# An eight-batch attention and expert block on one core: another order of calls, value tiles filled on ScalarE, a cleared tile multiplied in early gaps

## The chip, the core and the metric

One core of a Trainium2 chip runs the whole block in one launch. The metric is the device time in microseconds (us) of an execution; a profile of one execution shows every instruction of the five engines: TensorE (PE, with its weight loads PEld), VectorE (DVE), ScalarE (ACT), GpSimd (POOL) and SyncE (SP). Each engine has its own queue and takes it in order; semaphores tie them together.

## The reference

The input is 8 batches of 256 tokens of 128 features, float32. Each batch is normalised (xn) and goes into two branches that are added to it:

```
xn  = layernorm(x)
A   = softmax(q k^T / sqrt(128)) ; y = A summed with v as written, fc, bias
out0 = layernorm(xn + y) * gamma + beta
h   = rms(xn) ; 16 heads of 8 ; q, k = rms per head
ao  = causal softmax(q k^T / sqrt(8)) v, projected by wo
x1  = xn + ao (features 32 to 127 only) ; xf = rms(x1)
w   = top-2 weights of softmax(xf gate^T) over 4 experts
out1 = x1 + w0 gelu(e0) + w1 silu*linear(e1) + w2 (three gelu layers) + w3 (two gelu layers)
x + out0 + out1
```

In the first branch the reference's einsum sums attention over its keys and values over their tokens apart, so that it is a row sum of the softmax times one projected vector (fc_row).

## The kernel before

All weights and all batches stay in SBUF. The work is cut into some 70 small steps of a batch n: Python functions, each of which emits the instructions of one engine with the waits that they need. For each engine one long list of calls, written out by hand, sets the order in which the steps of all 8 batches are mixed: `batches()` for TensorE and VectorE, plain lists for GpSimd and ScalarE. The lists keep two or three batches in flight.

The steps of a batch, in the order in which its data flows:

- VectorE `ln_statistics`, `ln_moments`; GpSimd `ln_variance`, `ln_pow` and, for the second scale, `h_square`, `h_mean`, `h_eps`, `h_pow`; VectorE `ln_normalise` makes xn. TensorE `x_turn` transposes it, ScalarE `x_copy` takes it out of PSUM.
- TensorE `qkv_project(n, j)` for the two halves of the tokens, ScalarE `qkv_copy`; GpSimd `v_copy` puts the values into a tile `v_aug`, 32 columns for a head: 8 values, then a column of ones. VectorE `qk_square`, `qk_mean`, `rsqrt_input`, `rsqrt_guess`, four `cubic_` and three `newton_` steps, `qk_norm`. TensorE `qk_turn`, ScalarE `q_copy` and four `k_copy`.
- For each of 4 groups g of 4 heads: TensorE `scores(n, g)`, ScalarE `exp_group(n, g)`, GpSimd `mask(n, g)` (128x1024 elements in place), TensorE `weigh_v(n, g)`. VectorE `pv_turn`, `heads_inverse`, `heads_divide`, `ao_turn`; TensorE `wo_project`; VectorE `residual`; ScalarE `x1_square`; GpSimd `x1_pow`; VectorE `residual_scale` makes xf.
- The first branch: TensorE `q0_project`, `a0_scores(n, j)`; VectorE `a0_max`; ScalarE `a0_softmax`; VectorE `a0_inverse`, `a0_weight`; TensorE `fc_row`; VectorE `h0_sum`, `h0_statistics`, `h0_moments`, `h0_norm`; GpSimd `biased` and `h0_variance` to `h0_add`, then `x1_add`, which completes acc.
- Experts: TensorE `xf_turn`, `gate`, `e1_first`, `e1_second`, `l1_layer`, `l2_layer`, `l3_layer`, `e0_up`, `e3_in`, `e3_up_layer`, with ScalarE's gelu or tanh behind each and VectorE's `e1_gate` and `e1_product`; the small gate steps on VectorE; TensorE `down(n, j)`, and VectorE's `down(n, j, e)`, which adds the four weighted experts into acc. SyncE stores acc.

Results of TensorE go to four PSUM banks that many steps share in turn, beside the four banks of the scores. A step claims its bank when the result before it in that bank has been read:

```
"QKV0": "a", "QKV1": "a", "QKT": "a", "PV0": "a", "PV1": "a",
"XT": "b", "Q0T": "b", "S00": "b", "S01": "b", "FC": "b", "XFT": "b", "GATE": "b", "WO": "b",
"E1A": "even", "L1": "even", "L2": "even", "L3": "even", "DN0": "even",
"E1B": "odd", "E0": "odd", "D3": "odd", "U3": "odd", "DN1": "odd",
```

(S00 and S01 are the results of `a0_scores`, PV0 and PV1 those of `weigh_v`, DN0 and DN1 those of `down`.) A second list of the same calls, for inputs whose scores could overflow, is skipped at run time by a flag that VectorE computes first (`bound_scores`).

Of the kernel before, what the change touches and what calls it, by code (L numbers as in the profile page):

```python
# [30 lines left out]
def fused_block(nc: bass.Bass, x, cols, rows, w_proj, w_first, w_up, w_mid, w_down, out):  # L31
# [15 lines left out]
    with ExitStack() as ctx:  # L47
# [122 lines left out]
        def _(pe):  # L170
# [260 lines left out]
            def batches():  # L431
                x_turn(0); qkv_project(0, 0); fold_weights(); q0_project(0); qkv_project(0, 1); a0_scores(0, 0)
                a0_scores(0, 1); x_turn(1); qk_turn(0); q0_project(1); find_maxima(0); scores(0, 0); x_turn(2)
                qkv_project(1, 0); scores(0, 1); qkv_project(1, 1); fc_row(0); scores(0, 2); a0_scores(1, 0)
# [2 lines left out]
                a0_scores(2, 0); scores(1, 1); qkv_project(2, 1); a0_scores(2, 1); scores(1, 2); weigh_v(1, 0)
                xf_turn(0); weigh_v(1, 1); scores(1, 3); gate(0); l1_layer(0); e3_in(0); weigh_v(1, 2); x_turn(4)
                weigh_v(1, 3); e1_first(0); e3_up_layer(0); qk_turn(2); wo_project(1); l2_layer(0); e0_up(0)
                fc_row(2); find_maxima(2); scores(2, 0); l3_layer(0); e1_second(0); xf_turn(1); qkv_project(3, 0)  # L440
                scores(2, 1); e3_in(1); gate(1); down(0, 0); down(0, 1); q0_project(3); scores(2, 2)
# [955 lines left out]
```

## Time and profile before

| | us |
|---|---|
| median of 3 runs | 233.01 (232.93 to 233.16) |
| the execution that was profiled | 233.21 |
| its span, first to last instruction | 231.5 |
| TensorE / ScalarE / VectorE / GpSimd busy in it | 199.3 / 170.2 / 153.4 / 107.7 |

The profile's rows give times in us from the start of the span. In the timeline, instructions of one line that follow each other are merged (x2), and the bracket tells how long the engine was idle before them and what ended it. A group's row gives the busy time, the mean duration in ns of one, and the idle time ahead of the group.

### The profile page before, as it was taken

To read this page: it belongs to the slowest core of one execution; us is meant where nothing else is said; L and a number is where in the kernel's file an instruction comes from. 1 tells how busy PE (TensorE), PEld (TensorE's weight loads), DVE (VectorE), ACT (ScalarE), POOL (GpSimd) and SP (SyncE) were. 2 spreads that over 40 slices of the span, in tenths; PEclk is the share of its full clock that TensorE was granted. 3 is DMA by queue.
4 is the path that set the end of the run, shared out by engine and by line. 5 is a ranking of instruction groups with operands and counts; after the bars stand their busy time and mean duration, and the time that the engine had idled before them with its cause. 6 is when DMAs were issued, how large, how long until landed. Compare 5 with 4: busy or idle time off the path is not lost. (4 is left out here: it accounts for less than half of the span.)

```text
span 231.5 us, 5985 instructions
## 1 busy us (share of the span) xinstructions
PE 199.3 (86%) x2132; PEld 145.4 (63%) x2132; DVE 153.4 (66%) x534; ACT 170.2 (74%) x288; POOL 107.7 (47%) x190
## 2 busy tenths in 40 slices
PE   0557765989999998898999899999999999969892
PEld 0325433656868765765777678667786786747682
DVE  6453489279837881597669486797479847843354
ACT  2225843778998989997989998899999677636610
POOL 6851587865381715251476266515622536720000
PEclk9985999599999999999999999999999999999999
DMA  5930000000000000000000000000000000000001
GB/s 130 385 97 1 4 0 0 3 1 3 0 1 3 25 0 0 3 25 1 1 3 27 0 0 3 27 0 4 0 25 0 4 0 25 3 0 0 1 3 52
DMA packets 5393, 5.00 MB, mean 22 GB/s; under 512 B 498, under 2 KB 4850, under 8 KB 5362
## 3 DMA queue, kind: packets, MB, share of 16 engines
q1 hardware_dynamic: 5072, 4.39, 5.8%
q8 instruction: 19, 0.31, 0.5%
q10 hardware_dynamic: 290, 0.20, 0.4%
q14 instruction: 12, 0.10, 0.1%
HBM read 3.54 MB, written 1.05 MB: 20 GB/s over the span
## 5 line engine op out<-in xcount | busy, mean ns | idle before, releaser
L563 POOL TENSOR_SCALAR_AFFINE_SELECT probs<-probs 128x1024 f32<-128x1024 f32 x32 | 35.3, 1102 | 49.2 <-ACT probs L724 48.9
L724 ACT ACTIVATE probs<-scores_ps 128x1536 f32<-128x1536 f32 x32 | 46.4, 1449 | 6.9 <-PE scores_ps L246 6.6
L246 PEld LDWEIGHTS scores_ps<-qT,kT 32*128 32x128 f32 x512 | 24.8, 195 | 15.4 <-issue 11.8
L246 PE MATMUL scores_ps<-qT,kT 32*128 32x128 f32 (+1 forms) x512 | 31.7, 363 | 3.1 <-ACT probs L724 3.0
L360 PE MATMUL even_ps<-l_h,mid 128*128 128x256 f32 x128 | 31.8, 391 | 1.1 <-DVE e_s L1029 1.1
L360 PEld LDWEIGHTS even_ps<-l_h,mid 128*128 128x128 f32 x128 | 23.0, 189 | 6.8 <-DVE e_s L1029 1.7
L778 ACT ACT_TABLE_LOAD x18 | 23.1, 1283 | 2.3 <-PE even_ps L360 1.8
L333 PE MATMUL odd_ps<-xfT,up 128*128 128x256 f32 x80 | 21.8, 387 | 0.2 <-DVE e_h L1040 0.2
L271 PE MATMUL a_ps<-probs,v_aug 128*32 128x256 f32 x256 | 20.3, 389 | 1.5 <-DVE pv_rows L1048 1.4
L778 ACT ACTIVATE l_h<-even_ps 128x512 f32<-128x512 f32 x24 | 14.4, 599 | 8.7 <-PE even_ps L360 6.8
L1235 DVE SCALAR_TENSOR_TENSOR acc<-even_ps,wts,acc 128x96 f32<-128x96 f32 x32 | 10.2, 318 | 14.2 <-PE even_ps L392 11.7
L333 PE MATMUL even_ps<-xfT,up 128*128 128x256 f32 x64 | 17.8, 400 | 0.4 <-DVE e_s L1029 0.2
L333 PEld LDWEIGHTS odd_ps<-xfT,up 128*128 128x128 f32 x80 | 14.5, 190 | 3.1 <-DVE e_h L1040 0.8
L216 PE MATMUL a_ps<-qkvT,xnT 128*128 128x384 f32 x32 | 15.2, 558 | 0.6 <-ACT xnT L742 0.6
L284 PE MATMUL b_ps<-xnT,q0T 128*128 128x256 f32 x32 | 11.2, 435 | 4.0 <-ACT a_exp L731 4.0
L731 ACT ACTIVATE a_exp<-b_ps,a_negmax 128x256 f32<-128x256 f32 x16 | 7.5, 472 | 9.1 <-DVE a_negmax L1122 9.1
L830 ACT ACTIVATE kT<-a_ps,k_rows 128x256 f32<-128x256 f32 x32 | 13.7, 493 | 0.0
L186 PE MATMUL b_ps<-ident,xn 128*128 128x128 f32 x16 | 4.0, 336 | 11.0 <-DVE xn L1222 8.1
L333 PEld LDWEIGHTS even_ps<-xfT,up 128*128 128x128 f32 x64 | 11.0, 189 | 3.4 <-ACT l_h L778 1.3
L724 ACT ACT_TABLE_LOAD x10 | 12.8, 1283 | 0.2
L275 PE MATMUL a_ps<-probs,v_aug 128*32 128x128 f32 x256 | 12.9, 273 | 0.0
L1048 DVE STREAM_TRANSPOSE pv_rows<-a_ps 128x512 f32<-128x512 f32 x16 | 11.3, 704 | 1.8 <-PE a_ps L275 1.8
(149 smaller groups left out, 433.3 us busy)
## 6 DMA issues: line engine op xcount, KB each, us to landing
x_sb<-in_x SPq DMA_DIRECT2D x8, 128.0 KB, 6.5
out<-acc SPq DMA_DIRECT2D x8, 128.0 KB, 1.8
mid<-in_mid SPq DMA_DIRECT2D x1, 640.0 KB, 7.4
up<-in_up SPq DMA_DIRECT2D x1, 578.0 KB, 6.3
downs<-in_down SPq DMA_DIRECT2D x1, 512.0 KB, 8.2
first<-in_first SPq DMA_DIRECT2D x1, 320.0 KB, 5.6
proj<-in_proj SPq DMA_DIRECT2D x1, 192.0 KB, 2.9
row<-in_rows ACTq DMA_DIRECT2D x1, 192.0 KB, 4.8
```

The source lines that it names most:

```text
L216: T.matmul(ps[:, 0:3 * D], xnT[n % X_COPIES][:, j * P:(j + 1) * P], qkvT[:], start=True, stop=True).then_inc(full_sem(fill), 1)
L246: ins = T.matmul(ps, kT[p][rows, g, kt * P:(kt + 1) * P], qT[p][rows, kt * P:SEQ], start=kt == 0, stop=kt == 1 and not searching, tile_pos ...
L271: T.matmul(rows, v_aug[p][:, 0, GROUPS * lane + g, :], probs[g][:, lane, 0:SEQ], start=True, stop=False, tile_position=(0, 32 * lane))
L275: ins = T.matmul(rows[:, P:SEQ], v_aug[p][:, 1, GROUPS * lane + g, :], probs[g][:, lane, SEQ:SEQ + P], start=False, stop=True, tile_positi ...
L284: T.matmul(ps, q0T[n % Q0_COPIES][:, j * P:(j + 1) * P], xnT[n % X_COPIES][:], start=True, stop=True).then_inc(full_sem(fill), 1)
L333: ins = T.matmul(ps[:, m * SEQ:(m + 1) * SEQ], wT[:, m * P:(m + 1) * P], xfT[n % XF_COPIES][:], start=True, stop=True)
L360: ins = T.matmul(ps[:, m * SEQ:(m + 1) * SEQ], wT[:, at_col:at_col + P], src[:, ci, :], start=(ci == 0), stop=(ci == HC - 1))
L563: nc.gpsimd.affine_select(out=own, in_=own, compare_op=ALU.is_ge, fill=0.0, base=0, pattern=[[0, LANES * TILES], [1, P]], channel_multipli ...
L724: nc.scalar.activation(probs[g][:, :, 0:SEQ + P], scores_ps[:, :, 0:SEQ + P], ACT.Exp).then_inc(s["exp_done"], 1)
L778: nc.scalar.activation(dst[n % 2][:].rearrange("p c q -> p (c q)"), ps_of(fill), ACT.Gelu).then_inc(read_sem(fill), 1)
L830: nc.scalar.activation(kT[n % HEAD_COPIES][:, g, :], ps_of("QKT")[:, SEQ:2 * SEQ], ACT.Copy, scale=k_rows[:, g:g + 1]).then_inc(s["k_copie ...
L1048: V.transpose(pv_rows[n % 2][:, 2 * pair:2 * pair + 2].rearrange("p g n e -> p (g n e)"), ps_of(fill)).then_inc(read_sem(fill), 1)
```

## The change

All four long lists are written anew. Beside that:

- The three value tiles were cleared and given their ones by VectorE (`clear_heads`); now ScalarE fills them whole with ones (`fill_heads`), and columns 9 to 31 of a head, which nobody uses, hold ones instead of zeros.
- VectorE clears a tile `spare` first of all, and TensorE multiplies it with itself into the odd bank (`keep_busy`): three times before the flag, and at four places early in its list, ten more. Nobody reads the result.
- The row constants (192 KB) are loaded by SyncE's queue behind x of batch 2 and no longer by ScalarE's queue; x of batch 4 is loaded ahead of mid and downs.

```
+            def keep_busy(count):
+                for _ in range(count):
+                    T.matmul(banks["odd"][:, 0:SEQ], spare[:, 0:P], spare[:], start=True, stop=True)
...
-                x_turn(0); qkv_project(0, 0); fold_weights(); q0_project(0); qkv_project(0, 1); a0_scores(0, 0)
-                a0_scores(0, 1); x_turn(1); qk_turn(0); q0_project(1); find_maxima(0); scores(0, 0); x_turn(2)
...
+                keep_busy(4); fold_weights(); x_turn(0); keep_busy(1); qkv_project(0, 0); x_turn(1); qkv_project(0, 1)
+                q0_project(0); qkv_project(1, 0); a0_scores(0, 0); qkv_project(1, 1); keep_busy(3); x_turn(2)
+                keep_busy(1); q0_project(1); qkv_project(2, 0); a0_scores(0, 1); qk_turn(0); fc_row(0); find_maxima(0)
+                scores(0, 0); a0_scores(1, 0); qkv_project(2, 1); scores(0, 1); a0_scores(1, 1); qk_turn(1)
+                scores(0, 2); x_turn(3); keep_busy(1); scores(0, 3); weigh_v(0, 0); weigh_v(0, 1); fc_row(1)
+                weigh_v(0, 2); weigh_v(0, 3); find_maxima(1); scores(1, 0); q0_project(2); qkv_project(3, 0)
...
-                wo_project(7); l3_layer(6); e3_up_layer(6); e1_first(6); xf_turn(7); e1_second(6); gate(7)
-                l1_layer(7); e3_in(7); e1_first(7); e3_up_layer(7); l2_layer(7); e0_up(7); l3_layer(7); e1_second(7)
-                down(6, 0); down(6, 1); down(7, 0); down(7, 1)
+                weigh_v(7, 3); e0_up(6); l2_layer(6); wo_project(7); e3_up_layer(6); e1_first(6); e1_second(6)
+                xf_turn(7); l3_layer(6); e3_in(7); gate(7); down(6, 0); down(6, 1); a0_scores(7, 1); e1_first(7)
+                e3_up_layer(7); fc_row(7); l1_layer(7); e1_second(7); l2_layer(7); e0_up(7); l3_layer(7); down(7, 0)
+                down(7, 1)
+            pe.wait_ge(s["spare_ready"], 1)
+            keep_busy(3)
...
             load_x(2)
+            sp.dma_start(row_set[:], rows[0:3 * D].partition_broadcast(P)).then_inc(s["rows_in"], 16)
             load_x(3)
             sp.dma_start(up[:], w_up).then_inc(s["up_in"], 16)
+            load_x(4)
...
-            search_constants(); ln_variance(0); ln_pow(0); h_square(0); h_mean(0); h_eps(0); x1_start(0); h_pow(0)
+            search_constants(); ln_variance(0); ln_pow(0); h_square(0); ln_variance(1); h_mean(0); ln_pow(1); h_eps(0)
+            h_square(1); h_pow(0); x1_start(0); h_mean(1); x1_start(1); h_eps(1); biased(0); h_pow(1); biased(1)
...
+            def fill_heads(p):
+                if p == 0:
+                    act.wait_ge(s["halves_ready"], 1)
+                nc.scalar.activation(v_aug[p][:].rearrange("p j h e -> p (j h e)"),
+                                     minus_half[:, 0:1].to_broadcast([P, TILES * HEADS * 32]), ACT.Copy, scale=-2.0
+                                     ).then_inc(s["heads_filled"], 1)
...
-            x_copy(0); qkv_copy(0, 0); weights_copy(); q0_copy(0); qkv_copy(0, 1); a0_softmax(0, 0); a0_softmax(0, 1)
-            x_copy(1); q_copy(0); k_copy(0, 0); k_copy(0, 1); q0_copy(1); k_copy(0, 2); k_copy(0, 3); exp_group(0, 0)
...
+            fill_heads(0); fill_heads(1); fill_heads(2); weights_copy(); x_copy(0); qkv_copy(0, 0); x_copy(1)
+            qkv_copy(0, 1); q0_copy(0); qkv_copy(1, 0); a0_softmax(0, 0); qkv_copy(1, 1); x_copy(2); q0_copy(1)
+            qkv_copy(2, 0); a0_softmax(0, 1); q_copy(0); k_copy(0, 0); k_copy(0, 1); k_copy(0, 2); k_copy(0, 3)
+            exp_group(0, 0); qkv_copy(2, 1); a0_softmax(1, 0); exp_group(0, 1); q_copy(1); k_copy(1, 0); k_copy(1, 1)
+            a0_softmax(1, 1); exp_group(0, 2); k_copy(1, 2); k_copy(1, 3); x_copy(3); exp_group(0, 3); exp_group(1, 0)
...
-                ln_normalise(0); scale_projection(); head_scales(); ln_statistics(1); ln_moments(1); ln_normalise(1)
-                qk_square(0); a0_max(0, 0); qk_mean(0); ln_statistics(2); rsqrt_input(0); ln_moments(2)
...
+                head_scales(); scale_projection(); ln_statistics(1); ln_moments(1); ln_normalise(0); ln_normalise(1)
+                ln_statistics(2); qk_square(0); ln_moments(2); qk_mean(0); a0_max(0, 0); rsqrt_input(0)
+                rsqrt_guess(0); ln_normalise(2); cubic_square(0); cubic_product(0); cubic_terms(0); cubic_correct(0)
+                newton_square(0); newton_error(0); newton_correct(0); qk_square(1); qk_norm(0); qk_mean(1)
+                ln_statistics(3); rsqrt_input(1); a0_max(0, 1); rsqrt_guess(1); ln_moments(3); cubic_square(1)
+                cubic_product(1); cubic_terms(1); a0_inverse(0); a0_weight(0); cubic_correct(1); h0_sum(0)
...
-            for p in range(HEAD_COPIES):
-                clear_heads(p)
+            V.memset(spare[:], 0.0).then_inc(s["spare_ready"], 1)
             bound_scores()
             ln_statistics(0)
```

## Rows read from the trace of the kernel before

**Rows 1.** The page's head: span, busy time of each engine.

```profile
span 231.5 us, 5985 instructions
PE 199.3 (86%) x2132; PEld 145.4 (63%) x2132; DVE 153.4 (66%) x534; ACT 170.2 (74%) x288; POOL 107.7 (47%) x190
```

**Rows 2.** Windows: stretch, length, busy us (instructions) of each engine, granted clock, DMA.

```profile
15.60:22.40 6.80, 4.50 (x18) 2.69 (x22) 3.82 (x19) 2.78 (x10) 2.15 (x6) 0.50 0.00 1
39.50:46.30 6.80, 6.76 (x42) 4.09 (x45) 2.68 (x10) 5.30 (x14) 5.16 (x9) 0.50 0.01 2
...
22.93:41.94 19.01, 13.19 (x152) 8.17 (x153) 13.76 (x43) 10.82 (x20) 13.31 (x20) 0.94 0.00 1
41.94:196.50 154.56, 148.53 (x1682) 109.81 (x1682) 109.39 (x381) 137.64 (x223) 75.40 (x116) 0.99 0.02 7
196.50:231.50 35.00, 26.94 (x266) 21.11 (x262) 18.06 (x63) 14.26 (x25) 5.91 (x10) 0.99 0.04 10
```

**Rows 3.** Waits, 0 to 50 us: who waited for whom, us, times, longest.

```profile
DVE h L1140 <- PE b_ps L293: 6.9, 1, 6.9
...
PE b_ps L284 <- ACT a_exp L731: 4.0, 2, 2.2
...
PE b_ps L186 <- ACT a_exp L731: 2.9, 2, 2.3
```

**Rows 4.** Timeline, 0 to 28 us: start, duration, engine, line, operation.

```profile
6.89 0.60 DVE L1222 TENSOR_SCALAR xn<-x_sb,ln_mv,ln_rstd 128x128 f32<-128x128 f32 x2 [1.20 <-POOL ln_rstd L655]
...
8.27 0.38 ACT L742 ACTIVATE xnT<-b_ps 128x256 f32<-128x256 f32 x1 [4.77 <-PE b_ps L186]
...
8.80 1.65 PE L216 MATMUL a_ps<-qkvT,xnT 128*128 128x384 f32 x2 [0.56 <-ACT xnT L742]
...
13.13 0.58 ACT L760 ACTIVATE qkv<-a_ps,h_scale 128x384 f32<-128x384 f32 x1 [0.27 <-PE a_ps L216]
...
18.70 0.69 DVE L1114 TENSOR_TENSOR qk_n<-qkv,qk_y 128x512 f32<-128x512 f32 x1
...
23.06 0.81 PE L216 MATMUL a_ps<-qkvT,xnT 128*128 128x384 f32 x2
...
24.52 0.94 PE L246 MATMUL scores_ps<-qT,kT 32*128 32x256 f32 x16 [0.65 <-ACT probs L724]
```

**Rows 5.** Timeline, 28 to 56 us.

```profile
37.34 0.69 DVE L1114 TENSOR_TENSOR qk_n<-qkv,qk_y 128x512 f32<-128x512 f32 x1
...
41.94 1.45 ACT L724 ACTIVATE probs<-scores_ps 128x1536 f32<-128x1536 f32 x1 [0.26 <-PE scores_ps L246]
```

**Rows 6.** Groups of the whole span: table loads, a gelu, the memsets.

```profile
L778 ACT ACT_TABLE_LOAD x18 | 23.1, 1283 | 2.3 <-PE even_ps L360 1.8 <-PE odd_ps L333 0.2
...
L778 ACT ACTIVATE l_h<-even_ps 128x512 f32<-128x512 f32 x24 | 14.4, 599 | 8.7 <-PE even_ps L360 6.8 <-PE even_ps L333 1.7
...
L901 DVE MEMSET v_aug<- 128x1024 f32 x3 | 2.7, 912 | 1.4 <-PEq L1386 1.1
...
L816 ACT ACT_TABLE_LOAD x1 | 1.3, 1283 | 0.0
```

**Rows 7.** DMA issues from 1.70 to 1.85 us, us to landing.

```profile
row<-in_rows ACTq DMA_DIRECT2D x1, 192.0 KB, 4.8
x_sb<-in_x SPq DMA_DIRECT2D x1, 128.0 KB, 5.3
```

**Rows 8.** Timeline, 196 us to the end.

```profile
197.90 1.39 DVE L1165 TENSOR_SCALAR h0n<-h,h_mv,h_rstd 128x128 f32<-128x128 f32 x2
...
198.11 1.10 POOL L563 TENSOR_SCALAR_AFFINE_SELECT probs<-probs 128x1024 f32<-128x1024 f32 x1 [0.48 <-ACT probs L724]
```

**Rows 9.** TensorE's waits from 41.9 to 196.5 us.

```profile
PE scores_ps L246 <- ACT probs L724: 1.7, 4, 0.6
PE a_ps L271 <- DVE pv_rows L1048: 1.4, 2, 0.7
```

**Rows 10.** The chain that ended last: start, us, what.

```profile
224.26 1.56 PE even_ps L392 x32
```

More of the change, by code:

```diff
@@ L437, in batches @@
[L437 to L441, printed above, removed]
@@ new lines, in batches @@
+                scores(1, 1); wo_project(0); qkv_project(3, 1); a0_scores(2, 0); scores(1, 2); weigh_v(1, 0)
+                weigh_v(1, 1); a0_scores(2, 1); scores(1, 3); xf_turn(0); weigh_v(1, 2); l1_layer(0); gate(0)
+                e3_in(0); x_turn(4); weigh_v(1, 3); l2_layer(0); qk_turn(2); e3_up_layer(0); wo_project(1)
+                e1_first(0); e0_up(0); fc_row(2); find_maxima(2); scores(2, 0); e1_second(0); l3_layer(0); xf_turn(1)
+                qk_turn(3); scores(2, 1); gate(1); e3_in(1); q0_project(3); down(0, 0); down(0, 1); scores(2, 2)
@@ new lines, in batches @@
+                qkv_project(4, 1); x_turn(5); l3_layer(2); wo_project(3); e3_up_layer(2); qkv_project(5, 0)
+                q0_project(4); down(2, 0); xf_turn(3); qkv_project(5, 1); e3_in(3); l1_layer(3); e0_up(3); l2_layer(3)
+                gate(3); down(2, 1); a0_scores(4, 0); e1_first(3); qk_turn(4); e1_second(3); x_turn(6); find_maxima(4)
+                scores(4, 0); e3_up_layer(3); l3_layer(3); scores(4, 1); qk_turn(5); down(3, 0); down(3, 1)
+                scores(4, 2); weigh_v(4, 0); weigh_v(4, 1); scores(4, 3); a0_scores(4, 1); weigh_v(4, 2); fc_row(4)
@@ new lines, in batches @@
+                weigh_v(4, 3); find_maxima(5); scores(5, 0); q0_project(5); qkv_project(6, 0); scores(5, 1)
+                wo_project(4); qkv_project(6, 1); a0_scores(5, 0); scores(5, 2); weigh_v(5, 0); a0_scores(5, 1)
+                scores(5, 3); xf_turn(4); weigh_v(5, 1); e3_in(4); l1_layer(4); gate(4); weigh_v(5, 2); fc_row(5)
+                e0_up(4); l2_layer(4); x_turn(7); weigh_v(5, 3); e3_up_layer(4); qk_turn(6); l3_layer(4)
+                find_maxima(6); scores(6, 0); wo_project(5); e1_first(4); e1_second(4); q0_project(6)
@@ new lines, in batches @@
+                qkv_project(7, 0); scores(6, 1); a0_scores(6, 0); qkv_project(7, 1); down(4, 0); scores(6, 2)
+                down(4, 1); xf_turn(5); scores(6, 3); l1_layer(5); e0_up(5); gate(5); weigh_v(6, 0); weigh_v(6, 1)
+                l2_layer(5); weigh_v(6, 2); e3_in(5); a0_scores(6, 1); weigh_v(6, 3); e1_first(5); qk_turn(7)
+                e1_second(5); wo_project(6); find_maxima(7); scores(7, 0); e3_up_layer(5); l3_layer(5); fc_row(6)
+                scores(7, 1); q0_project(7); down(5, 0); down(5, 1); scores(7, 2); xf_turn(6); weigh_v(7, 0)
@@ L706, in _ @@
+            h0_add(7); x1_add(7)
         @block.scalar
@@ new lines, in _ @@
+            k_copy(4, 3); exp_group(4, 0); e3_up_gelu(3); l3_gelu(3); exp_group(4, 1); q_copy(5); k_copy(5, 0)
+            k_copy(5, 1); k_copy(5, 2); k_copy(5, 3); exp_group(4, 2); x_copy(6); exp_group(4, 3); a0_softmax(4, 1)
+            exp_group(5, 0); q0_copy(5); qkv_copy(6, 0); exp_group(5, 1); x1_square(4); qkv_copy(6, 1)
+            a0_softmax(5, 0); exp_group(5, 2); a0_softmax(5, 1); exp_group(5, 3); xf_copy(4); e3_in_gelu(4)
+            l1_gelu(4); gate_exp(4); e0_gelu(4); l2_gelu(4); x_copy(7); e3_up_gelu(4); q_copy(6); k_copy(6, 0)
```

277 lines of the change are left out of this document (120 added, 157 removed).

## The prediction

> **What bounds the kernel now.** I read the page first [rows 1]: TensorE (PE) is busy 199.3 of 231.5 us, ScalarE 170.2, VectorE 153.4, GpSimd 107.7. The execution that was profiled took 233.21 us, 1.71 more than its span; the median of the runs shown is 233.01. My sum is made against 231.5 and 233.21, and the 0.2 between that execution and the median goes off at the end, rounded away. A measurement of this kernel can tell about 0.2% (0.47 us) from no change.
>
> The mean hides three stages, so I read the windows next [rows 2]. I cut at two marks that exist in both orders, the first exponential of batch 1 and the end of the last scores of batch 7. In F, 0 to 41.94, TensorE waits a lot; in M, 41.94 to 196.5, it is busy 148.53 of 154.56 us; T, from 196.5, takes 35.0 with 26.94 busy, which leaves 23.8 busy in F. So F and T have the idle time, and M can only give 6.0 us unless matmuls leave it or run faster. They can run faster: between 15.6 and 22.4 and between 39.5 and 46.3 the granted clock is 0.50 [rows 2], the lower of its two levels (1.2 GHz), each time after TensorE had waited repeatedly [rows 3]. Before 12.2 the records call the clock full, but the first qkv_project took 1.65 us and a later one 0.81 [rows 4], so the start ran at the lower level too.
>
> Why TensorE waits in F is told by the waits up to 50 us [rows 3] and the timeline [rows 4, 5]. Bank b holds eight kinds of results one after another; a0_scores and x_turn wait there for a softmax (4.0 and 2.9 us), whose maximum stands in VectorE's queue. VectorE itself sat 6.9 us before h0_sum(0), waiting for fc_row(0), with qk_square(1) queued behind it. So qk_norm(1) starts only at 37.34 [rows 5], and nothing of batch 1 can be scored before. ScalarE was busy 10.82 of the 19.01 us from the first exponential of batch 0 to that of batch 1 [rows 2].
>
> **The change, part by part.**
>
> *Value tiles.* Three VectorE memsets of 0.91 us go [rows 6], a quarter-size one (at most 0.91) comes. Their replacement, three ScalarE fills of 1024 elements, I price between 0.60 (512 elements) and 1.45 (1536) [rows 5, 6], about 1.0 each. ScalarE's first operation came at 8.27, after a wait for TensorE [rows 4], so this costs nothing. If that cover were gone, 3 us of ScalarE at the start. VectorE reaches ln_statistics(0) up to 1 us earlier, but two things take that back: GpSimd is still in its constants, and ln_normalise(0) now stands behind ln_statistics(1), thus behind the landing of x of batch 1.
>
> *Transfers.* That landing was 5.3 us after its issue, while 192 KB of row constants, 4.8 us from issue to landing, ran beside it [rows 7]. The constants move behind x of batch 2 on SP, which may bring x of batch 1 half a microsecond forward, from about 7.0 to 6.5. Statistics take about 0.75, so ln_normalise(0) starts near 7.3 against 6.89 [rows 4]: 0.4 late (0.9 if the landing doesn't move). The fifth x passes mid and downs, needed much later: nothing.
>
> *Cleared matmuls.* Seven run before the first weights land, six later, each behind something and ahead of a call that waits. At full clock one costs about 0.5 (256 columns, where a qkv_project of 384 took 0.81 [rows 4]); 13 are 6.5 us, of which I put none on the path, because TensorE waits at those places. With that cover gone: the six later ones, 3.0.
>
> *The front.* The new order projects batches 1 and 2 before the first heads are turned, and issues x_turn(1) before any a0_scores, so the softmax wait of bank b no longer holds the transposes. I follow it with the durations of before. qkv_copy(0,1) ends near 12.0 where it ended at 13.71 [rows 4]. VectorE's chain from there to qk_norm(0) filled 5.7 us; it now has one qk_square more (0.7) and waits about 0.7 for ln_normalise(2), so qk_norm(0) ends near 18.9 against 19.39. a0_max(0,1), its softmax and q_copy(0) follow one by one; the first exponential starts near 23.5 against 22.93 [rows 2]. So far nothing is won but projections done early. From there ScalarE's queue decides. Its stretch to exp_group(0,3) holds what it held before, less one x_copy, one qkv_copy (0.58) and q0_copy(2): 10.82 less 1.5 is 9.3, end at 32.8 if it never waits. It could wait for qk_norm(1), which I find near 26.2, because qk_square(1) now precedes h0_sum(0); q_copy(1) is due at about 27.6. Then mask(0,3) 1.10 [rows 8], weigh_v and scores(1,0), at most 0.94 each [rows 4]: exp_group(1,0) near 35.8, against 41.94 [rows 5]. I allow 2 us for waits and for VectorE operations that still meet GpSimd: 37.7, **4.2 gained**. Bounds: 6.2, and nothing.
>
> *M.* Two qkv_project (about 0.7 each: 0.81 less what overlaps the next call) leave M at its front and q0_project(2), two thirds as wide, enters; a0_scores(7,0), a0_scores(7,1) and the half as wide fc_row(7) leave at its end, 1.1 by the same measure: 2.0 less. From 39.5 to 46.3 TensorE was busy 6.76 us at clock 0.50, without a gap [rows 2], 4.4 of it after 41.94; at full clock that is 2.2 less. ScalarE's switches between the exponential's and Gelu's tables, counted in the orders, fall from 37 to 33; the counted 37 and one at the start are the 38 loads of the trace (six groups, 18 loads in the first, 1 in the last), 1.28 us each [rows 6]. In M alone they fall from 34 to 28, 7.7 us of ScalarE's 137.64. That lies beside TensorE. What can come back is the idle time that ScalarE ended, mainly 1.7 before scores, and that VectorE ended, mainly 1.4 before weigh_v [rows 9]: zero to 6.0 in all, I take 1.5. **5.7 gained.** The new order also runs batch 3's experts in one block before batch 4's heads. By calls and mean durations, an estimate, TensorE has 25 us of work there and ScalarE 18, after a stretch in which ScalarE has 57 and TensorE 50. Were each stretch between two groups of scores paced by its busier engine, M would sum to 168 in the old order (it took 154.6) and to 162 in the new, so I charge that block nothing.
>
> *T.* a0_scores(7,·) and fc_row(7) enter (1.1), two table loads more (2.6), two a0_softmax (1.3); two of the four last down calls move ahead of batch 7's chain, 1.56 each in the chain of waits, 3.1 [rows 10]. All of it on the path: 36.9; only the gain: 31.9. Following the chain (three loads ahead of l2_gelu(6), then l3_layer(6), down(6,0), e1_first(7), e1_gate(7), l1, l2 and l3 of batch 7 on the one bank) I get 36.5, so **1.5 lost**.
>
> *Wide operations kept apart.* The only price that the trace shows: h0n took 1.39 us for two, and ended 0.08 after a GpSimd mask of 1.10 that began 0.21 into it [rows 8]; the like pair on xn took 0.60 at 6.89 [rows 4], so 0.8 was lost. The Trainium skill, page "SBUF — State Buffer", section "Who interferes with whom", says that a VectorE instruction with two SBUF inputs, or in a two-port mode, and a GpSimd instruction exclude each other for a whole instruction. By that rule every such meeting avoided returns its full wait; by the row alone I credit it where TensorE waited for VectorE.
>
> Sum: 231.5 − 4.2 − 5.7 + 1.5 = 223.1; with 1.71 outside the span 224.8. **224.8 us.**
>
> **Rivals.**
>
> *Apart means all of it (faster still).* VectorE's stretching, not ScalarE and the banks, holds the order together, and keeping the operations apart returns all idle time of M (4.5 more) and in T the 0.8 that h0n lost: 219.5. For it: VectorE is 13.76 of 19.01 busy in the front [rows 2]. Against: in M TensorE's largest wait for VectorE came to 1.4 us [rows 9]. The rule of the Trainium skill above, taken whole, would be this rival.
>
> *The clock falls anyway.* The cleared matmuls stand at a few places; behind a0_softmax(0,1) TensorE still idles about 2 us, and gaps of that length stood before each fall [rows 2, 3]. Then M keeps its 2.2 and the front loses 2.3: 229.3. This is also how the change fails to do what it says.
>
> *ScalarE's queue blocks (slower).* q_copy(1) and k_copy(1,·) now stand ahead of exp_group(0,2). If qk_norm(1) comes as late as before, 38.0, exp_group(0,2) follows at about 40.4, and from there to exp_group(1,0) is 7.3 by the same count, so 47.7: 5.8 late instead of 4.2 early, 224.8 + 10.0 = 234.8, and 237 if M also keeps its lower clock. It decides once qk_norm(1) ends after about 34. Against: qk_square(1) no longer stands behind the 6.9 us wait.
>
> *No change.* Front and M gain half, 5.0, and T loses that much: 233.2.
>
> **How the numbers follow.** Forecast 0.60, its own range 219.5 to 229; lock 0.10; clock 0.15; blocked queue 0.12; no change 0.03. The first three are faster: 0.85; slower 0.12; same 0.03. For 8 in 10 I cut below at 217.5, under the lock case, and above at 233, which leaves out the blocked queue and little else.
>
> **What would show it.** Right: exp_group(1,0) starts before 39; no stretch at clock 0.50 after about 25 us; 34 table loads; M of about 149 us; T of 35 to 37. Wrong: qk_norm(1) ends after 34 with ScalarE idle before q_copy(1); the clock at 0.50 between 25 and 46; TensorE idle over 9 us in M, above all between exp_group(3,3) and exp_group(4,0); acc of batch 7 waiting for GpSimd's x1_add(7) at the end.

## The result and the profile after

The changed kernel takes 224.06 us (median of 4 runs, 223.75 to 224.70) against 233.03 (232.93 to 233.16): a ratio of 0.9618, 95% interval 0.9597 to 0.9640. The forecast was 224.8, range 217.5 to 233.0. The total was hit; its terms were not. Of the runs below, those over 1.5% above the fastest of their kernel are left out of times and ratios (two of the kernel with fills on VectorE, one with Tanh).

The stages below are those of the profiled execution, the slowest of the four (224.70 us). The other three had a granted clock of 1.000 and spans of 222.0 to 222.4.

The page's head and its row of TensorE's granted clock (40 slices of 5.6 us, in tenths), to hold against [rows 1] and against the clock row of the kernel before, which stands first (slices of 5.8 us):

```profile
PEclk9985999599999999999999999999999999999999
...
span 223.0 us, 6031 instructions
...
PE 203.4 (91%) x2158; PEld 149.8 (67%) x2158; DVE 137.7 (62%) x529; ACT 167.6 (75%) x287; POOL 106.7 (48%) x190
...
PEclk9999999999999999999999999699999999999999
```

Windows at the prediction's two marks; the columns are those of [rows 2]:

```profile
0.00:34.58 34.58, 28.26 (x219) 19.24 (x220) 23.03 (x89) 21.62 (x45) 25.47 (x68) 1.00 0.32 104
34.58:187.27 152.69, 146.58 (x1674) 108.55 (x1676) 97.49 (x369) 128.27 (x212) 74.73 (x114) 0.99 0.02 7
187.27:223.00 35.73, 28.61 (x269) 22.00 (x268) 17.20 (x73) 17.74 (x31) 6.48 (x11) 0.99 0.04 10
```

Against [rows 2], F went from 41.94 to 34.58 (7.4 gained, 4.2 forecast), M from 154.56 to 152.69 (1.9 gained, 5.7 forecast), T from 35.00 to 35.73 (0.7 lost, 1.5 forecast). Two misses of 3.2 and 3.8 have cancelled each other.

The turning points of F in the timeline, to hold against [rows 4, 5]:

```profile
6.71 0.60 DVE L1234 TENSOR_SCALAR xn<-x_sb,ln_mv,ln_rstd 128x128 f32<-128x128 f32 x2 [0.57 <-POOL ln_rstd L666]
...
8.70 0.91 PE L222 MATMUL a_ps<-qkvT,xnT 128*128 128x384 f32 x2
...
11.23 0.58 ACT L778 ACTIVATE qkv<-a_ps,h_scale 128x384 f32<-128x384 f32 x1 [0.64 <-PE a_ps L222]
...
16.98 0.68 DVE L1126 TENSOR_TENSOR qk_n<-qkv,qk_y 128x512 f32<-128x512 f32 x1
...
21.37 1.45 ACT L742 ACTIVATE probs<-scores_ps 128x1536 f32<-128x1536 f32 x1
...
23.21 0.69 DVE L1126 TENSOR_TENSOR qk_n<-qkv,qk_y 128x512 f32<-128x512 f32 x1
...
34.58 1.45 ACT L742 ACTIVATE probs<-scores_ps 128x1536 f32<-128x1536 f32 x1 [3.21 <-PE scores_ps L252]
```

The first qkv_project ran at the full clock (0.91 us, where [rows 4] have 1.65). qk_norm(0) ends at 17.66 (forecast 18.9), the first exponential starts at 21.37 (23.5), qk_norm(1) ends at 23.90 (26.2), and exp_group(1,0) starts at 34.58 (35.8, and 37.7 with the allowance).

In M TensorE still idles 152.69 − 146.58 = 6.1 us, as much as before (6.0). Its waits there, to hold against [rows 9]:

```profile
PE b_ps L187 <- ACT a_exp L749: 1.5, 2, 1.3
PE scores_ps L252 <- ACT probs L742: 1.2, 3, 0.4
PE b_ps L299 <- ACT a_exp L749: 0.6, 1, 0.6
```

The waits for pv_turn are gone, but a transpose (L187) now waits 1.3 us on bank b for an a0_softmax. The timeline from 136 to 145 us shows that wait, the windows below it what followed:

```profile
136.55 0.70 PE L290 MATMUL b_ps<-xnT,q0T 128*128 128x256 f32 x2
...
137.45 1.45 DVE L1213 TENSOR_SCALAR xf<-x_sb,x_scale 128x128 f32<-128x128 f32 x2 [0.60 <-POOL x_scale L646]
...
137.73 1.09 POOL L574 TENSOR_SCALAR_AFFINE_SELECT probs<-probs 128x1024 f32<-128x1024 f32 x1
...
138.82 0.41 DVE L1134 TENSOR_REDUCE a_negmax<-b_ps 128x1 f32<-128x256 f32 x1
...
139.27 0.47 ACT L749 ACTIVATE a_exp<-b_ps,a_negmax 128x256 f32<-128x256 f32 x1 [1.76 <-DVE a_negmax L1134]
...
139.89 0.44 PE L187 MATMUL b_ps<-ident,xf 128*128 128x128 f32 x2 [1.30 <-ACT a_exp L749]
```

```profile
136.00:140.30 4.30, 2.60 (x40) 1.58 (x35) 3.40 (x6) 2.54 (x6) 4.30 (x6) 1.00 0.00 0
140.30:143.80 3.50, 3.50 (x22) 2.33 (x22) 1.02 (x4) 2.90 (x4) 1.53 (x3) 0.51 0.01 2
```

Read it from the top: a0_scores(5,1) ends at 137.25, and its maximum could follow, but VectorE holds the pair of residual_scale(4) (xf) for 1.45 us (it had itself waited 0.60 for x_scale(4) from GpSimd); the pair ends at 138.90, 0.08 after the mask that began beside it. The maximum, the softmax and xf_turn(4) are late one by one, TensorE idles 1.30 us, and the clock then stands at 0.51 for 3.5 us. The like pair xn took 0.60 at 6.71. So in the changed order too, one meeting of VectorE and GpSimd made a wait, and a fall of the clock came behind that wait. The same order with narrow masks (an experiment below) shows that the mask made it: there the second xf instruction took 0.34 us instead of 1.13, and the same transpose waited 0.35 instead of 1.30:

```profile
137.49 0.44 PE L187 MATMUL b_ps<-ident,xf 128*128 128x128 f32 x2 [0.35 <-ACT a_exp L749]
```

The fall of the clock is less sure to follow. Five of the traced kernels below wait 1.30 or 1.31 us at this transpose; in three of them (changed, no cleared multiplications, old transfers) the clock fell behind it, in two (fills on VectorE, order alone) it stayed at 1.00 throughout M.

### The profile page after: what moved, and what is told of

Same layout as the page of the kernel before. It is cut to its first block, busy times and chain, and to the rows that moved or that the text cites. A ratio compares the mean times of both kernels' runs of the same rounds, so it can differ in the third digit from the quotient of the medians.

```text
span 223.0 us, 6031 instructions
## 1 busy us (share of the span) xinstructions
PE 203.4 (91%) x2158; PEld 149.8 (67%) x2158; DVE 137.7 (62%) x529; ACT 167.6 (75%) x287; POOL 106.7 (48%) x190
## 4 chain that ended last, share of the span: by engine, by line
PE 50%; ACT 16%; issue 12%; DVE 12%; POOL 8%; POOLq 0%; ACTq 0%; DVEq 0%
PE even_ps L366 7%; PE scores_ps L252 6%; PE odd_ps L339 5%; PE even_ps L339 5%; PE a_ps L277 5%; ACT probs L742 4%; PE even_ps L398 4%; PE odd_ps L398 3%; PE odd_ps L382 3%; PE odd_ps L192 3%; PE a_ps L222 3%; POOL probs L574 2%; ACT L796 2%; DVE acc L1247 2%; PE a_ps L281 2%
## 5 line engine op out<-in xcount | busy, mean ns | idle before, releaser
L252 PE MATMUL scores_ps<-qT,kT 32*128 32x128 f32 (+1 forms) x512 | 29.9, 347 | 2.9 <-ACT probs L742 2.7
L252 PEld LDWEIGHTS scores_ps<-qT,kT 32*128 32x128 f32 x512 | 23.5, 184 | 11.9 <-issue 9.5
L366 PE MATMUL even_ps<-l_h,mid 128*128 128x256 f32 x128 | 30.7, 383 | 0.2 <-DVE e_s L1041 0.2
L366 PEld LDWEIGHTS even_ps<-l_h,mid 128*128 128x128 f32 x128 | 23.8, 190 | 4.6 <-ACT l_h L796 0.9
L339 PE MATMUL odd_ps<-xfT,up 128*128 128x256 f32 x80 | 22.9, 401 | 0.8 <-ACT u_h L796 0.8
L796 ACT ACT_TABLE_LOAD x16 | 20.5, 1283 | 1.0 <-PE odd_ps L339 0.3
L222 PE MATMUL a_ps<-qkvT,xnT 128*128 128x384 f32 x32 | 13.7, 509 | 1.1 <-ACT qkv L778 0.9
L339 PEld LDWEIGHTS even_ps<-xfT,up 128*128 128x128 f32 x64 | 11.8, 198 | 3.3 <-ACT l_h L796 0.8
L281 PE MATMUL a_ps<-probs,v_aug 128*32 128x128 f32 x256 | 13.2, 277 | 0.0
L281 PEld LDWEIGHTS a_ps<-probs,v_aug 128*32 128x32 f32 x256 | 8.5, 112 | 5.7 <-issue 0.4
L778 ACT ACTIVATE qkv<-a_ps,h_scale 128x384 f32<-128x384 f32 x16 | 9.3, 580 | 3.9 <-PE a_ps L222 3.7
L1134 DVE TENSOR_REDUCE a_negmax<-b_ps 128x1 f32<-128x256 f32 x16 | 6.7, 418 | 7.8 <-PE b_ps L290 7.7
```

The lines of the kernel that those rows point to most:

```text
L222: T.matmul(ps[:, 0:3 * D], xnT[n % X_COPIES][:, j * P:(j + 1) * P], qkvT[:], start=True, stop=True).then_inc(full_sem(fill), 1)
L252: ins = T.matmul(ps, kT[p][rows, g, kt * P:(kt + 1) * P], qT[p][rows, kt * P:SEQ], start=kt == 0, stop=kt == 1 and not searching, tile_pos ...
L281: ins = T.matmul(rows[:, P:SEQ], v_aug[p][:, 1, GROUPS * lane + g, :], probs[g][:, lane, SEQ:SEQ + P], start=False, stop=True, tile_positi ...
L339: ins = T.matmul(ps[:, m * SEQ:(m + 1) * SEQ], wT[:, m * P:(m + 1) * P], xfT[n % XF_COPIES][:], start=True, stop=True)
L366: ins = T.matmul(ps[:, m * SEQ:(m + 1) * SEQ], wT[:, at_col:at_col + P], src[:, ci, :], start=(ci == 0), stop=(ci == HC - 1))
L796: nc.scalar.activation(dst[n % 2][:].rearrange("p c q -> p (c q)"), ps_of(fill), ACT.Gelu).then_inc(read_sem(fill), 1)
```

## The experiments

All of them in one table: the stages of the profiled execution in us, cut as above, TensorE's busy time in M, and the ratio of the runs to the kernel before on the same chip, with its 95% interval. (In these sessions the kernel before took 232.5 to 235.7, so that a ratio is good to about half a per cent.)

| kernel | F | M | busy in M | T | ratio to before |
|---|---|---|---|---|---|
| before | 41.94 | 154.56 | 148.53 | 35.00 | 1 |
| changed | 34.58 | 152.69 | 146.58 | 35.73 | 0.9618 (0.9597 to 0.9640) |
| no cleared multiplications | 36.50 | 152.70 | 146.52 | 35.90 | 0.9722 (0.9671 to 0.9773) |
| fills on VectorE | 38.56 | 151.74 | 144.99 | 35.70 | 0.9650 (0.9575 to 0.9725) |
| old transfers | 35.41 | 152.86 | 146.57 | 35.53 | 0.9621 (0.9578 to 0.9665) |
| parts alone | 39.00 | 153.25 | 146.57 | 36.95 | 0.9826 (0.9760 to 0.9892) |
| order alone | 39.39 | 151.67 | 144.98 | 35.54 | 0.9792 (0.9726 to 0.9858) |
| new front, old rest | 35.43 | 153.35 | 145.45 | 35.42 | 0.9710 (0.9639 to 0.9781) |
| old front, new rest | 46.88 | 155.16 | 146.05 | 35.43 | 1.0203 (1.0132 to 1.0273) |
| before, narrow masks | 40.44 | 149.87 | 145.79 | 34.09 | 0.9664 (0.9601 to 0.9728) |
| changed, narrow masks | 33.98 | 149.86 | 144.57 | 35.66 | 0.9451 (0.9396 to 0.9506) |
| before, narrow masks, paced | 41.30 | 150.08 | 145.92 | 34.22 | 0.9736 (0.9685 to 0.9788) |
| before, Tanh for Gelu | 43.65 | 150.11 | 145.92 | 34.34 | 0.9811 (0.9746 to 0.9876) |
| scores(1,0) first | 32.58 | 156.65 | 149.59 | 35.67 | 0.9681 (0.9638 to 0.9724) |

**No cleared multiplications.** All 13 go: three ahead of the flag and ten at five places of TensorE's list (the section on the change counts four).

```diff
-keep_busy(4); fold_weights(); x_turn(0); keep_busy(1); qkv_project(0, 0); x_turn(1); qkv_project(0, 1)
+fold_weights(); x_turn(0); qkv_project(0, 0); x_turn(1); qkv_project(0, 1)
...
-keep_busy(3)
```

> The changed kernel without any of its 13 cleared multiplications; all else as in the change. Theory A (the order of calls gives the gain, the clock is a small part of it): 225 to 227 us; the clock stands at 0.50 in the first 8 us and perhaps once more before the first exponential of batch 1, which starts between 34.6 and 37. Rival C (the clock was most of the gain): 230 us or more, with a stretch at 0.50 between 20 and 46 us as in the kernel before. Rival D (the cleared multiplications cost time themselves): 222 to 223.5 us.

Measured: 227.37 us (226.90 to 228.34). F is 1.9 longer, M and T are as in the changed kernel. The windows of its F:

```profile
0.00:36.50 36.50, 23.63 (x193) 14.54 (x194) 23.08 (x89) 21.76 (x44) 26.20 (x68) 0.95 0.31 98
```

TensorE is busy 4.6 us less than in the changed kernel's F and still ends it 1.9 later, at a mean clock of 0.95 where the changed kernel had 1.00. So the cleared multiplications bring 1.9 us here, a fifth to a quarter of the whole gain (1.0 of 3.8 per cent by the ratios, 2.4 us), and not most of it. The total is 0.4 above theory A's range; F lies within it. The records show no 0.50 in the first 8 us, where the first qkv_project again took 1.65 us, but they show one from 22.5 to 25.9.

**Fills on VectorE.** VectorE's clear_heads comes back, ScalarE's fill_heads goes.

```diff
-fill_heads(0); fill_heads(1); fill_heads(2); weights_copy(); x_copy(0)
+weights_copy(); x_copy(0)
...
+for p in range(HEAD_COPIES):
+    clear_heads(p)
```

> The changed kernel, but VectorE clears the value tiles (three memsets, each followed by the small one of ones) ahead of its other work, as before the change, and ScalarE fills nothing. Theory A (the fills cost and bring nothing, since the first normalised tile waits for its input): the same as the changed kernel within 0.5 us, 223.8 to 224.7, with the first normalised tile starting at most 1 us later than 6.71. Rival E (VectorE's start is on the path): 1.5 to 3 us slower than the changed kernel, 225.5 to 227.

Measured: 226.39 us (224.92 to 227.76, 4 runs); the profiled execution has F at 38.56, 4.0 late. From the timeline of its first 10 us:

```profile
4.80 0.12 DVE L918 SCALAR_TENSOR_TENSOR qk_w<-qk_rows 1x8 f32<-1x8 f32 x1
...
6.33 3.77 PE L192 MATMUL odd_ps<-spare 128*128 128x256 f32 x8 [2.16 <-issue]
...
8.23 0.57 DVE L1232 TENSOR_SCALAR xn<-x_sb,ln_mv,ln_rstd 128x128 f32<-128x128 f32 x2
```

The expectation of no more than 0.5 us was wrong, for two reasons. VectorE's statistics start later (ln_statistics(0) at 5.21 and not at 2.93), so that xn comes at 8.23, 1.5 late. And the flag that VectorE computes (bound_scores, from qk_w) comes at 4.80 and not at 2.00, behind three memsets; TensorE's lists stand behind that flag, so it idles 2.16 us, and the next four cleared multiplications (x8: two records each) take 0.94 each, where one in the changed kernel took 0.60 at 7.97; they are still running when xn is there. x_turn(0) starts at 10.56, where it started at 7.75. In the kernel with the order alone, which has VectorE's fills and no cleared multiplications, it starts at 8.88: so of these 2.8 us about 1.1 come from the later xn and 1.7 from the multiplications behind the late flag. In the profiled F the clock also stood at 0.50 from 30.8 to 34.2. In runs with the clock full the loss was smaller (spans of 223.1 and 223.4, where the changed kernel at the full clock has 222.0 to 222.4), so its size hangs on the clock: 1 to 4 us, and the ratios alone can't tell it from nothing.

**Old transfers.** The row constants go back to ScalarE's queue, the fifth x behind the weights.

```diff
-sp.dma_start(row_set[:], rows[0:3 * D].partition_broadcast(P)).then_inc(s["rows_in"], 16)
...
+act.dma_start(row_set[:], rows[0:3 * D].partition_broadcast(P)).then_inc(s["rows_in"], 16)
```

> The changed kernel with the transfers of the kernel before: the row constants on ScalarE's queue at once, the fifth x behind the expert weights. Theory A (the moved row constants let x of batch 1 and the first weights land earlier, and the first normalised tile now stands behind batch 1's statistics): x of batch 1 lands near 7.0 instead of 4.5, the first exponential of batch 1 starts 1 to 2 us later than 34.6, and the whole takes 225 to 226.5. Rival H (the transfers are hidden): 223.8 to 224.6.

Measured: 225.28 us (224.20 to 225.83). ln_statistics(1) starts at 7.01 after a wait for the transfer, where the changed kernel starts it at 5.38; F is 0.8 longer, where 1 to 2 had been expected. The median lies in theory A's range, but by the ratio (0.9621 against 0.9618) no difference is shown, and the two of the six runs that had a full clock took 224.20 and 224.26, beside 223.75 to 224.11 in the changed kernel: rival H is not excluded. The 0.8 of F is all that can be said.

**Parts alone and order alone.** The first keeps the order of before and takes the fills, the transfers and 22 cleared multiplications; the second takes the new order with nothing else.

```diff
-x_turn(0); qkv_project(0, 0); fold_weights(); q0_project(0); qkv_project(0, 1); a0_scores(0, 0)
-a0_scores(0, 1); x_turn(1); qk_turn(0)
+keep_busy(4); x_turn(0); keep_busy(1); qkv_project(0, 0); fold_weights(); q0_project(0); qkv_project(0, 1)
+a0_scores(0, 0); keep_busy(3); a0_scores(0, 1); keep_busy(3); x_turn(1); qk_turn(0)
...
```

> The order of the kernel before on every engine, with the other parts of the change: ScalarE fills the value tiles, the transfers go in the changed order, and TensorE multiplies the cleared tile, 22 times in all, ahead of the calls for which it waited in the front of the kernel before. Theory A (the order gives most): 229.5 to 232, the clock full from the start and the 2.2 us of the lower clock after 41.94 given back, the first exponential of batch 1 still after 38. Rival C (clock, fills and transfers give most): 227 or less, with the first exponential of batch 1 before 37.

> The changed order of calls on every engine with nothing else of the change: VectorE clears the value tiles, the transfers go as before, no cleared multiplications. Theory A (the order gives most): 226 to 229, with the first exponential of batch 1 between 37 and 40. Rival C (clock, fills and transfers give most): 231 or more.

Measured: 230.54 us (229.09 to 230.91) and 228.85 us (228.32 to 230.09). F splits by the start of scores(0,0), read from the timelines:

| | scores(0,0) starts | from there to exp_group(1,0) |
|---|---|---|
| before | 21.46 | 20.5 |
| parts alone | 19.33 | 19.7 |
| order alone | 23.78 | 15.6 |
| changed | 20.37 | 14.2 |

The order makes the start 1.0 to 2.3 later and the stretch behind it about 5 shorter: 2.6 gained without the parts, 4.4 with them. The parts bring the start 2.1 to 3.4 forward and the rest 0.8 to 1.4: 2.9 to 4.8 gained. Neither alone gives 7.4. Both totals lie in theory A's ranges, yet of theory A and rival C both are wrong as "most of it": each has about half of F, and by the ratios 2.1 per cent for the order and 1.7 for the parts make up the 3.8. (T is 36.95 with the parts alone, since the clock fell to 0.50 there, from 201.0 to 204.4.)

**New front, old rest; old front, new rest.** The lists of both kernels are cut where exp_group(1,0) starts, and crossed.

```diff
-scores(1, 0); q0_project(2); qkv_project(3, 0); scores(1, 1); wo_project(0); qkv_project(3, 1); a0_scores(2, 0)
+scores(1, 0); q0_project(2); wo_project(0); a0_scores(2, 0); scores(1, 1); a0_scores(2, 1); scores(1, 2)
...
```

> The changed kernel up to the first exponential of batch 1 (its order, its ScalarE fills, its transfers, its cleared multiplications), and from there the order of the kernel before on all engines. Theory A (the gain lies in the front): 224.5 to 227 us, with the first exponential of batch 1 near 34.6 and the middle stretch at 153 to 155. Rival B (keeping wide operations apart pays throughout the middle): 229 us or more, with the middle stretch over 156.

> The kernel before up to the first exponential of batch 1 (its order, VectorE memsets, its transfers, no cleared multiplications), and from there the changed kernel's order. Theory A (the gain lies in the front): 231 to 233 us, with the first exponential of batch 1 near 42 and the middle stretch 152 to 154. Rival B (the gain lies in the order of the middle): 227 us or less, with the middle stretch under 149.

Measured: 226.87 us (225.95 to 228.16) and 238.97 us (238.27 to 239.50). The new front keeps its gain with the old rest, as theory A had it. The old front with the new rest is slower than both kernels, which no theory had. Its exp_group(1,0) starts at 46.88, 4.9 later than in the kernel before. In ScalarE's crossed list qkv_copy(2,0) and qkv_copy(2,1) stand ahead of it, and TensorE makes their projections only at 43.87 and 45.45. TensorE's waits from 43.34 to 202 us begin:

```profile
PE b_ps L186 <- ACT a_exp L729: 2.3, 2, 1.3
PE a_ps L216 <- ACT qkv L758: 1.3, 2, 0.7
...
PE b_ps L284 <- DVE x_sb L1189: 1.1, 1, 1.1
```

M is 155.16, 0.6 longer than with the old rest behind the same front, and TensorE idles 9.1 of it. So most of the loss, 4.9 of the 6 us between the two profiled executions, lies at the seam: the new rest counts on projections of batch 2 that the new front has made and the old one hasn't (the waits for qkv). How the new rest would do behind an old front that made them isn't shown. Behind the new front the new rest is worth about 1.6 (M of 151.7 with the order alone, at the full clock, against 153.35).

**Narrow masks, in both kernels.** One width changes.

```diff
-own = probs[g][:].rearrange("p l (n q) -> p (l n) q", q=SEQ)[:, :, 0:P]
+own = probs[g][:].rearrange("p l (n q) -> p (l n) q", q=SEQ)[:, :, 0:8]
...
-                       pattern=[[0, LANES * TILES], [1, P]], channel_multiplier=-1
+                       pattern=[[0, LANES * TILES], [1, 8]], channel_multiplier=-1
```

> The kernel before with GpSimd's 32 masks cut to 8 of every 128 columns, which leaves out most of the causal mask: the masks can then neither stretch VectorE's operations nor be waited for long. Theory A (meetings of GpSimd's masks with VectorE are a small part of the gain): 230 to 232, and 7 or more above the changed kernel with the same cut. Rival B (keeping wide operations apart is the gain): 227 or less, within 4 of the changed kernel with the same cut.

> The changed kernel with GpSimd's 32 masks cut to 8 of every 128 columns, which leaves out most of the causal mask. Theory A: 222 to 224, 7 or more below the kernel before with the same cut. Rival B (the changed order already keeps the masks out of VectorE's way, and that is the gain): 222 to 224 too, but within 4 of the kernel before with the same cut.

Measured: 226.20 us (225.51 to 227.07) and 221.27 us (221.26 to 221.30). Theory A's expectation for the kernel before was missed by 4. Rival B's total for it was met, but not its distance: the two narrow kernels are 4.9 apart, where B had at most 4 and A 7 or more, and 221.27 lies under the range that both had. The wide masks cost the kernel before 7.2 us (233.39 in that session) and the changed one 2.8 (7.8 and 3.9 by the ratios), and the difference between the two kernels falls from 9.0 to 4.9. The M of both, first the kernel before:

```profile
40.44:190.31 149.87, 145.79 (x1681) 108.55 (x1678) 99.84 (x382) 137.10 (x224) 55.43 (x118) 1.00 0.03 7
```

```profile
33.98:183.84 149.86, 144.57 (x1674) 107.76 (x1676) 93.29 (x367) 128.11 (x212) 53.70 (x113) 1.00 0.03 7
```

With narrow masks M is the same in both orders; VectorE is busy 9.6 us less in the M of the kernel before than with wide masks (109.39). So the new order is ahead in M only while the masks are wide, and F's difference stays (40.44 against 33.98). Not all of the 4.7 us that M loses in the kernel before is waiting: 2.7 is busy time, since the clock no longer falls at 39.5. Against the parts alone, which have the old order and the wide masks at the full clock (M of 153.25), the narrow masks bring 3.4.

**Narrow masks, paced.** Is it the mask's own duration or its meeting with VectorE?

```diff
 pool.wait_ge(s["exp_done"], GROUPS * n + g + 1)
+for k in range(26):
+    nc.gpsimd.memset(ticks[:, 26 * (GROUPS * n + g) + k:26 * (GROUPS * n + g) + k + 1], 0.0)
```

> The kernel before with the narrow masks (8 of every 128 columns, so most of the causal mask is left out), and ahead of each mask 26 GpSimd memsets of one column, which should take the 0.8 us by which the narrow mask is shorter, while they touch hardly any memory. Theory M (VectorE is stretched by meeting the wide mask): the time stays near that of the narrow masks, 225.5 to 228. Theory L (the mask's own duration counts, as a wait of TensorE and as time in GpSimd's queue): back to 231 to 233.

Measured: 227.60 us (227.35 to 227.79). GpSimd's time in M is back, TensorE's M is not:

```profile
41.30:191.38 150.08, 145.92 (x1680) 108.44 (x1678) 101.59 (x382) 137.13 (x224) 74.66 (x819) 1.00 0.03 8
```

GpSimd is busy 74.66 us there, as before (75.40), a mask ends on the average 1.29 us after its exponential in both kernels, and M is 150.08, where wide masks gave 154.56 (153.25 at the full clock): the time that a mask takes in GpSimd's queue is not what M paid for. What this kernel doesn't do is keep VectorE free. The excess of VectorE's durations over the median of each form (longer by over 60 ns), summed over the trace, is 18.5 us before, 5.0 with narrow masks and 12.9 with the paced ones (9.3 where records that overlap count once), so a good part of the meetings is back. By the ratios 1.7 of the 7.8 us comes back. So the mask's own duration is ruled out as the main cause. That the meeting has the rest is argued from this and shown only for single waits, such as the one at xf_turn(4).

**Before, Tanh for Gelu.** No switch of ScalarE's tables is left.

```diff
-nc.scalar.activation(dst[n % 2][:].rearrange("p c q -> p (c q)"), ps_of(fill), ACT.Gelu
+nc.scalar.activation(dst[n % 2][:].rearrange("p c q -> p (c q)"), ps_of(fill), ACT.Tanh
```

> The kernel before with Tanh in place of Gelu, which changes the experts' activation and needs no switch of ScalarE's tables: some 36 loads of 1.28 us leave ScalarE, about 28 of them in the middle stretch. Theory A (in the middle they lie beside TensorE, which is the bound): the middle stretch falls by 2 us at most, to 152.5 or more, the tail by 2 to 4, the whole to 227 to 230.5. Rival F (ScalarE paces the middle, so that fewer loads are worth most of their time): the middle under 150.5, the whole under 226.

Measured: 229.44 us (229.37 to 229.86, 3 runs). M:

```profile
43.65:193.76 150.11, 145.92 (x1682) 108.80 (x1684) 108.27 (x381) 94.13 (x189) 75.73 (x116) 1.00 0.03 7
```

The whole is in A's range, but M is under F's bound of 150.5, so the number alone speaks for F; its parts don't. ScalarE is busy 43.5 us less than in [rows 2] (94.13 against 137.64), and TensorE's idle time in M falls from 6.0 to 4.2, by 1.8. The other 2.6 is busy time: the fall of the clock came ahead of the mark here (F's mean clock 0.85, M's 1.00), and F is 1.7 longer. The expectation forgot that a fall can move over the mark. T is 0.7 shorter, where it had 2 to 4. 43.5 us of ScalarE return 1.8 of TensorE's idle time (2.5 against the parts alone); by proportion, an estimate, the changed order's 9.4 would return 0.4 to 0.5, not 1.5. M comes to 150.1 here with wide masks, as it does with narrow ones: either relief is enough for it, so the masks alone are not what held M at 153.

**scores(1,0) first.** An attempt at a faster kernel: ScalarE idles 3.21 us ahead of exp_group(1,0), so its scores go ahead of the last weigh_v of batch 0, and two cleared multiplications ahead of xf_turn(4).

```diff
-scores(0, 3); weigh_v(0, 0); weigh_v(0, 1); fc_row(1); weigh_v(0, 2); weigh_v(0, 3); find_maxima(1); scores(1, 0)
+scores(0, 3); weigh_v(0, 0); weigh_v(0, 1); find_maxima(1); scores(1, 0); fc_row(1); weigh_v(0, 2); weigh_v(0, 3)
...
-scores(5, 3); xf_turn(4)
+scores(5, 3); keep_busy(2); xf_turn(4)
```

> The changed kernel with the first scores of batch 1 moved ahead of fc_row(1), weigh_v(0,2) and weigh_v(0,3) on TensorE, and two more cleared multiplications ahead of xf_turn(4), where the clock fell in the profiled execution of the changed kernel. Theory A (behind the front TensorE is the bound, so only its idle time comes back): the first exponential of batch 1 starts near 32.6, no stretch at clock 0.50 after the start, and the whole takes 223.0 to 223.8. Rival G (the front's 2 us go through to the end): 222.2 or less. Rival N: no change from the changed kernel, 223.8 to 224.4.

Measured: 226.62 us (225.19 to 226.78), slower than the changed kernel and than all three expectations. exp_group(1,0) starts at 32.58 as expected, and the clock no longer falls at xf_turn(4); but M is 156.65. The timeline from 37 us, and a window behind it:

```profile
37.42 2.25 POOL L574 TENSOR_SCALAR_AFFINE_SELECT probs<-probs 128x1024 f32<-128x1024 f32 x2
...
37.49 2.26 DVE L1234 TENSOR_SCALAR xn<-x_sb,ln_mv,ln_rstd 128x128 f32<-128x128 f32 x2
39.67 0.34 DVE L1204 TENSOR_TENSOR x_sb<-b_ps,xn 128x192 f32<-128x192 f32 x1
...
40.07 0.70 PE L290 MATMUL b_ps<-xnT,q0T 128*128 128x256 f32 x2 [1.75 <-DVE x_sb L1204]
```

```profile
40.10:46.90 6.80, 6.55 (x74) 3.95 (x78) 3.57 (x11) 4.09 (x11) 5.90 (x10) 0.75 0.00 0
```

Two masks, now due at once, run back to back for 2.25 us, and the pair of ln_normalise(4), begun 0.07 after the first, takes 2.26 instead of 0.60. residual(0) stands behind it, a0_scores(2,0) waits 1.75 us for bank b, and then the clock is at a mean of 0.75 for 6.8 us (at 0.50 from 41.6 to 45.1). F is 2.0 shorter and M 4.0 longer than in the changed kernel, but the mark has moved with the edit: 2.9 us of TensorE's work (busy 25.3 in F, where the changed kernel has 28.3) now lie behind it, in M, which has 3.0 more busy time. F and M together are 2.0 longer, and 1.9 of that is idle time of TensorE; the wait of 1.75 is the longest in M. The whole takes 1.5 (by the ratios) to 2.6 us more. No version that beats both kernels was found.

## Why the prediction came out right

**The total was right by two wrong terms.** F was under-sized by 3.2 and M over-sized by 3.8. That the forecast lies within 0.1 us of the profiled execution, and within 0.8 of the median, is luck.

*F, 4.2 forecast, 7.4 measured.* The term "the front" credited the order alone with 4.2; it gives 2.6 by itself and 4.4 behind the parts. What failed is that the parts were priced at next to nothing. "Value tiles: so this costs nothing" looked at what ScalarE pays. Its gain on VectorE, "up to 1 us earlier", was 2.0 (ln_statistics(0) at 2.93, before at 4.95), and it was not taken back: the first xn came at 6.71, forecast 7.3, and comes 1.5 later with VectorE's fills in the same order. It also left out bound_scores, which stood behind the memsets and holds TensorE's whole list. "Cleared matmuls: none on the path" was right as a cost and left out the gain: the prediction saw that the first qkv_project ran at the lower level (1.65 against 0.81 [rows 4]) and put the clock into M's sum only. Without the cleared multiplications F is 1.9 longer. "Transfers, half a microsecond" was 1.6 or more (ln_statistics(1) at 5.38, with the old transfers at 7.01), and worth 0.8 of F. From the first exponential to exp_group(1,0) the forecast had 12.3 and the trace has 13.2, so 0.9 of the allowance of 2 us was needed; the start is 2.1 early.

*M, 5.7 forecast, 1.9 measured.* At the full clock TensorE's busy time in M is 146.6 in the order of before (parts alone) and 145.0 in the new one (order alone): "work leaving" is 1.6, forecast 2.0, and "clock" is 148.53 − 146.57 = 2.0, forecast 2.2. Both steps hold as busy time. That less work makes M shorter holds with the wide masks alone: with narrow ones TensorE has 1.2 less to do in the new order (144.57 against 145.79) and M is the same. "Idle given back", 1.5, failed: TensorE idles 6.1 as before. It leaned on ScalarE's 9.4 us, worth about half a microsecond by the estimate from the Tanh kernel, and on VectorE's waits, whose place the wait at xf_turn(4) took. And the profiled execution has a new fall of the clock, 146.58 − 144.98 = 1.6, which the other three runs don't have. So 1.6 + 2.0 − 1.6 − 0.1 = 1.9 in the profiled execution; the other three were 0.6 to 1.0 shorter as a whole, and their stages weren't traced.

*T, 1.5 lost forecast, 0.7 measured.* TensorE's work grew by 1.7 (26.94 to 28.61) and its idle time shrank by 0.9; T has five table loads where it had three, the two more that were forecast (34 in all).

**The rivals.** "Apart means all of it" had a tenth of the chance and has near half of the gain: 9.0 − 4.9 = 4.1 us of the difference hang on the wide masks, part of it by the clock, which doesn't fall at 39.5 in the narrow kernel before. The prediction credited meetings only "where TensorE waited for VectorE" by the row [rows 9]; what it missed is that a stretched operation delays the ones behind it in VectorE's queue, so that the wait is booked on ScalarE's softmax or a residual, and that a fall of the clock can come behind such a wait. The rival's 219.5 isn't reached: the changed order keeps meetings (the excess of VectorE's durations is 18.5 before and 7.5 after), and even with narrow masks it takes 221.27. "The clock falls anyway" happened in one run of four, in M, for 1.6 us of busy time. "ScalarE's queue blocks" did not: qk_norm(1) ended at 23.90. Of the signs to look for, M of 149 and, in the profiled execution, no stretch at the lower level after 25 us were wrong; exp_group(1,0) before 39, 34 loads, T of 35 to 37 and under 9 us of idle time in M were right.

**What stays open.** A part of the wide masks' 7.2 us may be their duration (the paced kernel brought back 1.7 by the ratios and still met VectorE). Why the clock fell behind the wait at xf_turn(4) in some runs and not in others isn't known. How the parts' gains in F (1.9, 4.0 and 0.8 by single profiles, 4.8 together) overlap wasn't taken apart.

## What to carry to other kernels

Cut the forecast and the traces at the same marks: a right total can stand on wrong stages. In the first microseconds, ask of each small operation what flag or branch stands behind it, and charge the clock's level there too. If an edit moves a mark, look at the busy time on both sides of it before reading a stage's time. An order that keeps two engines apart is good for one set of due times: a shift of 2 us ahead of it can bring the meetings back, and a wait that they cause is paid twice where the clock falls behind it.
